# A graph layer and a mixture of experts on one core: where the rows behind each expert's list are filled, by whom, and from which counts

## The reference

```python
# x: 3125 nodes x 256, 50000 edges; 8 experts, the best 2 for each node
x = x + gnn(layernorm(x), edges, W1_l, W1_r, b1, W2_l, W2_r, b2)     # two graph layers (mean over neighbours)
tokens = layernorm(x)
probs = softmax(tokens @ router_w.T)
rw, re = top_k(probs, 2); rw = rw / max(sum(rw), 1e-12)
ffn = tokens
for e in range(8):
    h = gelu(tokens @ w1[e] + b1[e])
    ffn = ffn + combine[:, e:e+1] * (h @ w2[e] + b2[e])
return x + ffn
```

## Time and profile before

| | us |
|---|---|
| median of 3 runs | 577.2 (576.48 to 577.6) |
| the profiled execution | 576.17 |
| its span, first to last instruction | 574.3 |
| TensorE busy in the span | 549.4 (96%) |
| VectorE busy | 369.2 (64%) |
| ScalarE busy | 225.1 (39%) |
| GpSimd busy | 183.8 (32%) |

### The profile page before, as it was taken

The page is one execution under the profiler, slowest core; times in us unless marked ns, Lnnn a source line. Parts: engine busy times, 40 slices in busy tenths (PEclk is TensorE's granted clock), DMA queues, the critical chain, the costliest instruction groups (busy, mean ns, idle before and its releaser), DMA issues.

```text
span 574.3 us, 11279 instructions
## 1 busy us (share of the span) xinstructions
PE 549.4 (96%) x3023; PEld 331.2 (58%) x3024; DVE 369.2 (64%) x1259; ACT 225.1 (39%) x426; POOL 183.8 (32%) x180
## 2 busy tenths in 40 slices
PE   4999999999999999999989999999999988999994
PEld 3545555555555555555435555555554777888883
DVE  5998677676766766766245576677788765444442
ACT  4666844453443534535100100000002644565563
POOL 3760000000000000000012033444436778787886
PEclk9999999999999999999999999999999999999998
DMA  7521121011110111101373134866324697778775
GB/s 256 156 86 56 56 65 56 29 56 42 42 56 30 55 38 47 54 29 57 58 240 96 60 93 140 244 210 218 112 93 164 179 259 139 130 117 144 122 119 66
DMA packets 64348, 61.30 MB, mean 107 GB/s; under 512 B 11281, under 2 KB 62334, under 8 KB 64302
## 3 DMA queue, kind: packets, MB, share of 16 engines
q1 hardware_dynamic: 47422, 44.84, 25.6%
q0 software_dynamic: 11200, 14.40, 13.7%
q10 hardware_dynamic: 5680, 1.49, 1.2%
HBM read 32.34 MB, written 29.30 MB: 107 GB/s over the span
## 4 chain that ended last, share of the span: by engine, by line
PE 68%; issue 11%; DMA 9%; POOL 4%; DVE 4%; POOLq 3%; ACT 0%; SPq 0%; DVEq 0%; ACTq 0%
PE bank L1515 23%; PE counts_ps L1515 14%; PE bank L1430 8%; PE counts_ps L752 7%; PE bank L1505 7%; DMA out<-adj 6%; POOL xs_dram L668 2%; POOLq L696 2%; PE counts_ps L1662 2%; PE bank L1675 2%; DMA y<-y_dram 2%; PE bank L1420 1%; POOLq L701 1%; PE bank L1498 1%; PE bank L1600 1%
## 5 line engine op out<-in xcount | busy, mean ns | idle before, releaser
L1515 PE MATMUL bank<-y,adj 128*128 128x512 f16 x625 | 154.7, 379 | 0.4 <-ACT zt L1752 0.4
L1515 PE MATMUL counts_ps<-y,adj 128*128 128x512 f16 x625 | 144.2, 379 | 1.9 <-DMA y<-y_dram 1.9
L759 ACT ACTIVATE adj<-counts_ps 128x1000 f32 (+1 forms) x80 | 80.2, 1005 | 58.7 <-PE counts_ps L752 58.7
L1515 PEld LDWEIGHTS counts_ps<-y,adj 128*128 128x128 f16 x625 | 60.5, 101 | 64.5 <-DMA y<-y_dram 4.2
L1515 PEld LDWEIGHTS bank<-y,adj 128*128 128x128 f16 x625 | 57.9, 97 | 59.5 <-issue 13.7
L645 POOL IOTA onehots<- 128x8 int32 x1 | 0.1, 143 | 224.9 <-PE counts_ps L752 224.9
L708 POOL DMA_INDIRECT out<-adj x40 | 62.5, 1563 | 15.3 <-DMA out<-adj 12.4
L1662 PE MATMUL counts_ps<-adj 128*128 128x256 f32 x240 | 56.9, 381 | 2.4 <-ACT adj L1874 2.4
L738 DVE TENSOR_TENSOR onehots<-iota,lo_t 125x1024 f16<-125x1024 f16 x80 | 54.9, 686 | 1.7 <-issue 0.9
L752 PEld LDWEIGHTS counts_ps<-onehots 125*128 125x128 f16 x640 | 42.5, 98 | 23.0 <-ACT adj L759 10.8
L738 DVE TENSOR_TENSOR onehots<-iota,key_t 125x1000 f16<-125x1000 f16 x80 | 53.9, 674 | 0.0
(11 more groups left out here) (292 smaller groups left out, 673.2 us busy)
## 6 DMA issues: line engine op xcount, KB each, us to landing
adj<-xs_dram SPq DMA_DIRECT2D x31, 264.0 KB
rows<-z_dram SPq DMA_DIRECT2D x49, 128.0 KB
z_dram<-zt SPq DMA_DIRECT2D x33, 128.0 KB, 1.7
adj<-in_L_ffn_w SPq DMA_DIRECT2D x16, 256.0 KB, 3.3
rows<-in_x SPq DMA_DIRECT2D x24, 128.0 KB
out<-yo SPq DMA_DIRECT2D x24, 128.0 KB
y_dram<-yo SPq DMA_DIRECT2D x23, 128.0 KB, 1.7
y<-y_dram SPq DMA_DIRECT2D x4, 640.0 KB, 6.8
```

The costliest lines, as they stand in the source:

```text
L759: nc.scalar.activation(adj[:, :, bass.ds(at, GW * WD)].rearrange("p b (h d) -> p b h d", d=WD), counts_ps[:, 2 * (group % 2):2 * (group % ...
L1515: last = te.matmul(to, adj[:, b, t * P:(t + 1) * P], y[:, b, :], start=(b == 0), stop=(b == NT - 1))
```

## The change

- The end of each expert's list is taken after batch 5 (tiles up to 22), not after the last batch: `end_i` is written in `place(NB - 2)` from `hist[:, NB - 1, :]`.
- Tiles 23 and 24 (181 nodes, `LATE`) can still lengthen a list by at most 181 rows. So a filler covers 256 + 181 rows, rounded up to 448 (`PAD_ROWS`), written as four rows in each of 112 partitions' share.
- The scatters of tiles 23 and 24 overwrite some of these rows. So GpSimd waits for all eight fillers to have landed (`padded`) before those scatters; the wait stands behind the first two adds.
- All eight fillers are issued by SyncE: 0 and 1 after the output of the last tile, 2 to 4 after the rows of unit 4, 5 to 7 after the rows of unit 5. ScalarE issues none.

```diff
+    LATE = N - FIRST_OF[NB - 1] * P
+    PAD_ROWS = PAIR + LATE + (-LATE) % 64
...
-                engine.dma_start(xs_dram[bass.ds(end, PAIR), :].rearrange("(h p) n -> p h n", p=P),
-                                 pad_t.rearrange("p (h n) -> p h n", h=1).to_broadcast((P, 2, XW))
+                engine.dma_start(xs_dram[bass.ds(end, PAD_ROWS), :].rearrange("(h p) n -> p h n", h=4),
+                                 pad_t[0:PAD_ROWS // 4, :].rearrange("p (h n) -> p h n", h=1)
+                                 .to_broadcast((PAD_ROWS // 4, 4, XW))
                                  ).then_inc(S["padded"], 16)
...
             sp.dma_start(out[(NT - 1) * P:, :], uo[0:LAST, :]).then_inc(S["u_out"], 16)
+            pad_experts(sp, range(0, 2))
             next_rows(4, row_of(4))
+            pad_experts(sp, range(2, 5))
             next_rows(5, row_of(5))
             row = row_of(6)
-            pad_experts(sp, range(0, 2))
+            pad_experts(sp, range(5, NE))
             next_rows(6, row)
-            row = row_of(7)
-            pad_experts(sp, range(2, 4))
-            next_rows(7, row)
+            next_rows(7, row_of(7))
...
             for q in range(AHEAD):
                 add_half(0, q, True)
+            pool.wait_ge(S["padded"], 16 * NE)
             for t, j in to_scatter[FIRST_OF[NB - 1]:]:
                 scatter(t, j)
...
-                if j == NB - 1:
+                if j == NB - 2:
                     link(last)
-                    v.tensor_copy(end_i, hist[:, NB, :]).then_inc(S["ends"], 1)
+                    v.tensor_copy(end_i, hist[:, NB - 1, :]).then_inc(S["ends"], 1)
...
-                if 1 <= i <= 2:
-                    pad_experts(act, range(2 * i + 2, 2 * i + 4))
```

More of the change, by code:

```diff
@@ L79, in build @@
     COEF, CHOSEN, NODE_ID = D, D + TOPK, D + 2 * TOPK
+    assert FIRST_OF[NB - 1] * P + PAD_ROWS <= REGION
     assert NCH <= P and NCH * CHUNK == E and ALL_ROWS <= P and ALL_ROWS * ALL_COLS == E
```

## The result

The changed kernel takes 588.75 us (median, 588.17 to 590.66), the kernel before on the same chips 576.84 us. The ratio is 1.0221 (1.02 to 1.0241): 2% slower, and 2.2 us above the range that the prediction gave.

The account below looks back on a forecast made before the run. GpSimd's full queue was taken to bound the end: scatters 6.6 us later, less 0.5 us of gaps, + 6.1 us, span 580.4, median 583.3 us. Bounds were 579.2 to 586.4, the eight-in-ten range 578.3 to 586.6.

Parts of the forecast that it names:

- the time at which the last filler lands: Landing before the scatters of tiles 23 and 24: 467.0 from 5.2 MB at 341 GB/s, bounds 463.9 to 470.1.
- What bounds the kernel: Expert stage: GpSimd and TensorE full; the time hangs on when GpSimd's 54 adds start, + 105.4 us, + 2.5 us.
- Part 1: The fillers themselves: eight transfers of 448 rows, 3.78 MB instead of 2.16 MB, each byte costing as before.
- Part 2: Fillers issued by SyncE from 450.85, 1.15 us apart, last at 461.1; ScalarE's relief worth 0 us while GpSimd is later.
- rival 3: Far slower: SyncE's value loads stretch under full DMA, 2.06 us steps, last filler lands 471.9; + 11 us, 588; chance 0.09.
- just in time: Unit 5's row load, queued behind fillers on SyncE, moves from 455.14 to about 457.6; TensorE wants the rows near 463.5.
- The 0.78 us after the landing: On GpSimd, the time from the last filler's landing until its next instruction starts; scatters then start at 467.8.
- the block of 5.13 us: GpSimd's four scatters of tiles 23 and 24, expected to take as long as before, 5.13 us.
- the adds at 1.855 us: GpSimd's adds: 1.55 us each plus 0.30 us read as issue cost, so the step of 1.855 us cannot shrink.
- What comes back: Gaps among GpSimd's 54 adds, 5.3 us in all: 0.5 us taken back, before the add at 482.91; bounds 0 to 1.5.
- a sign of being wrong: On GpSimd: gaps among the adds shrinking by more than 2 us would show the forecast wrong.
- Rivals 1 and 2: Rival 1: wait absorbed, 577.2 us, chance 0.10; rival 2: fillers land before GpSimd's wait, ScalarE's relief counts, 575.9, 0.07.

Follow-up runs that it names:

- the wait alone: Kernel before plus one line: GpSimd waits for all eight 256-row fillers ahead of the scatters of tiles 23 and 24; 585.39 us, ratio 1.0153.
- both full forms: Changed kernel with fillers written from 128 partitions: three rows each (384 rows), 584.97 us, ratio 1.0127; four rows each (512 rows), 585.83 us, ratio 1.0149.
- With the wait out: Changed kernel without GpSimd's wait; fillers start 192 rows further on, 13 blocks of 128 rows written early from GpSimd; 597.18 us, ratio 1.0368.
- the loads moved ahead: Changed kernel with SyncE loading all eight ends and the row addresses of units 4 to 6 before the first filler; 589.35 us, ratio 1.0233.
- relief for ScalarE: Kernel before with all eight fillers issued by SyncE, four before the rows of unit 6, four before those of unit 7; 578.59 us, ratio 1.0021.
- The size alone: Kernel before with fillers of 448 rows in 112 x 4 form, nothing moved and no wait on GpSimd; 587.72 us, ratio 1.019.

## Why the prediction was wrong

The direction and the mechanism held. The step that failed is the time at which the last filler lands, a term of the sum: 467.0 forecast, 475.2 measured, above even the upper bound of 470.1. Of these 8.2 us, 1.1 is that this execution reached tile 20's scatter later. In the prediction's own terms (bytes over rate from 451 on), 5.9 MB moved and not 5.2, which is 1.9 us at 341 GB/s, and they moved at 242 GB/s and not at 341, which is the other 6.3. The span came out 6.2 us over the forecast and not 8.2, because 2.0 us more came back behind the wait than I took.

- **What bounds the kernel: right.** From the first add behind the last scatters to the end of the span it is 105.2 to 105.5 us in the changed kernel, the wait alone and both full forms, wherever the stream starts, and taking all fillers away gained nothing. One row I misread: the 1.31 us before the last add is labelled "issue" in the earlier trace rows, so nothing there shows a wait for a landing.
- **Part 1, "I cost a byte as before": wrong.** The rate that I took, 341 GB/s, came from transfers of 128 partitions and from the fullest 7 us of the trace; the 10 us around them, 461 to 471, moved 297. From 455 to 470 the changed kernel moved 254 GB/s, and even the full form only 295 and 309. The changed kernel with more bytes in the full form is 2.9 us faster.
- **Part 2, SyncE's issues: wrong.** The eleven register loads ahead of the last filler took 10.2 us; at the 0.27 us of a quiet load in the kernel before (`L437 SPq TENSOR_LOAD <-onehots x4: 267/270/836, 457.2 to 463.7; - x4`) they would be 3.0. The last issue is at 470.87, not 461.1. I had used the loaded spacing of 2.06 us only for rival 3, though the forecast itself assumed a full DMA. In the full form, too, the waits are still 9.5 and 12.0 us. By counting only two row loads between fillers I also left out the address load of unit 6, which stands ahead of the last three fillers (1.3 us).
- **Rows of unit 5 "just in time": wrong.** They were issued 7 us later than I said, and TensorE stood 4.46 us. GpSimd's wait covered it here. With the wait out TensorE stood 3.75 us for rows and GpSimd 6.52 us for ScalarE; how much of that is these rows is not shown.
- **The 0.78 us after the landing, the block of 5.13 us, the adds at 1.855 us: right** (0.79, 5.15, no two adds closer than 1.85).
- **What comes back: too small.** The first add moved by 481.14 - 466.32 = 14.8 us, the span by 12.3, so 2.5 us came back where I took 0.5, with 1.5 as the bound. Over the 54 adds the idle time fell from 21.3 to 18.4 us, by 2.9 where I had called more than 2 a sign of being wrong. I took back only the gap before 482.91. The largest of the kernel before stands ahead of it, 1.45 us for a half that ScalarE had not weighed, and is gone in the changed kernel; so a gap from late units was there, though I had said that most were not. The line before, then the two groups of the changed kernel:

```profile
473.10 1.55 POOL L706 DMA_INDIRECT out<-adj  x1 [1.45 <-ACT adj L1889]
```

```profile
L712 POOL DMA_INDIRECT out<-adj x40 | 62.9, 1573 | 13.9 <-DMA out<-adj 9.0 <-issue 4.3 <-ACT adj L1894 0.6
L710 POOL DMA_INDIRECT out<-adj x14 | 22.0, 1568 | 4.5 <-issue 2.1 <-DMA out<-adj 2.1 <-ACT adj L1894 0.3
```

- **Rivals.** Rival 3 comes nearest, at 588 us, and I gave it 0.09. Its place was right: loads on SyncE stretched, and unit 5's rows came late. As the whole cause it falls, since the loads moved ahead gave 589.35 us, and its number is luck in part: it had the last filler land at 471.9, 3.3 us too early, and left the 2.5 us that came back at 0.5. Its "then unit 8's rows come late as well" was no cost: TensorE stood 0.22 us for them. Rivals 1 and 2 are out: the wait was not absorbed (585.4 us for the wait alone), and relief for ScalarE gave nothing (578.6).
- **What I had no term for.** Large fillers also delay the landings of adds and ScalarE's own issues. The size alone costs 11 us with no wait for fillers on GpSimd. The two ways don't add up: 11 us by size, 9 by the wait, 12 together. In the changed kernel the adds start after the fillers have landed, and none behind the wait stood longer than 1.25 us.

What stays open: why a filler from fewer than 128 partitions drains more slowly; how the changed kernel's late landing, and the 9.5 us of wait that remain in the full form, split between SyncE's stretched chain and the rate, since the two drive each other and no run separates them; and what the early place on SyncE costs by itself, since no run has it with fillers of 256 rows.

## What to carry to other kernels

A new wait costs what is queued behind it on its engine: find out first whether that queue is full, by counting instructions times their step over a long stretch, and take the end from the queue's start. Price a transfer by its form as well as its bytes, and if the forecast has DMA full, take the issue steps and register loads of the loaded stretch, too. Before a transfer is moved for a gain, bound the gain by leaving the transfer out: here it was nothing.

## What the runs showed of the hardware

- The same 384 rows of 1056 bytes for each filler, written from 128, 96 and 64 partitions (3, 4 and 6 rows each), gave 579.8, 587.5 and 585.8 us, while all traffic from 461 to 471 moved 296, 268 and 248 GB/s with a full DMA share. 112 partitions were slow with 3 rows (584.2 us) and with 4 (587.7).
- The issue of such a transfer on SyncE took 620 ns (median of four) from 64 partitions with six rows each, 390 from 128 with two and 346 from 96 with four. Which of the two numbers makes the difference, no run shows.
- A load of one number into a register of SyncE took 0.26 to 0.28 us with DMA quiet and up to 2.21 us in the changed kernel's full stretch. It is not only the engine that issues most: in the kernel before the same loads took up to 1.41 us on ScalarE and 1.55 us on GpSimd.
